# Two-layer graph network and expert layer: the path for unsorted edges left out, and the last group of nodes cut to its own rows

## The reference, cut to what matters

```python
# x (6250, 512) float32; src, dst (100000,), sorted by dst
def sage(h, W_self, W_neigh, b):
    agg = segment_sum(h[src], dst, 6250)             # 100000 rows of 512 floats are gathered
    deg = segment_sum(ones, dst, 6250)
    return relu(h @ W_self + agg / max(deg, 1) @ W_neigh + b)
x = x + sage(sage(layernorm(x), ...1), ...2)         # two layers
xf = layernorm(x)
topv, topi = top_k(xf @ Wg, 2)                       # 8 experts, 2 for each node
y_e = layernorm(relu(xf @ W1[e] + b1[e]) @ W2[e] + b2[e]) * gamma[e] + beta[e]
x = x + sum over the 2 experts of softmax(topv) * y_e
```

## Time and profile before

| | us |
|---|---|
| median of three runs | 3189.15 |
| the profiled execution | 3192.86 |
| its span | 3191.1 |
| first stage, up to the first gather | 108.9 |
| first layer, first gather to the second layer's first | 1151.6 (108.9 to 1260.5) |
| second layer, first to last gather | 1110.1 (1260.5 to 2370.6) |
| first row of the experts' stage asked for | 2417.4 |

### The profile page before, as it was taken

How to read it: one execution, slowest core, us unless ns; L and a number is a source line. 1 busy time by engine, 2 the same in 40 slices (tenths; PEclk the granted TensorE clock), 3 DMA queues, 4 the chain that set the end, 5 groups by cost and what they waited for, 6 DMA issues and landing times.

```text
span 3191.1 us, 66577 instructions
## 1 busy us (share of the span) xinstructions
PE 2713.7 (85%) x12191; PEld 2108.6 (66%) x12192; DVE 2280.9 (71%) x5226; ACT 1727.3 (54%) x3193; POOL 2189.5 (69%) x2216
## 2 busy tenths in 40 slices
PE   1488878887889987899999999999996999899997
PEld 0366666666667765677777677777774777777775
DVE  7567666766667775888888888888875666666665
ACT  3455545545556654655656566555553555555554
POOL 0577777777777776777777777777753556555665
PEclk9988888888889998989899899888887999999998
DMA  7788888778877776777777777777765554555443
GB/s 276 230 256 267 270 273 268 254 254 267 257 247 227 213 215 222 231 231 231 235 236 234 234 230 234 227 233 224 235 196 157 136 135 75 132 133 135 73 80 63
DMA packets 234835, 664.22 MB, mean 208 GB/s; under 512 B 46602, under 2 KB 48196, under 8 KB 227612
## 3 DMA queue, kind: packets, MB, share of 16 engines
q0 software_dynamic: 151712, 465.58, 52.3%
q10 hardware_dynamic: 60768, 127.43, 11.2%
q1 hardware_dynamic: 22300, 70.69, 6.1%
HBM read 551.72 MB, written 111.83 MB: 208 GB/s over the span
## 4 chain that ended last, share of the span: by engine, by line
PE 36%; POOL 28%; issue 12%; DMA 11%; ACTq 5%; DVE 4%; ACT 2%; SPq 2%; DVEq 1%; POOLq 0%
POOL store_all L685 27%; PE ps L1619 22%; PE ps L1646 6%; DMA store_all<-h_scratch,srcT 5%; PE ps L1647 4%; ACTq L375 2%; DMA out<-store_all,idx_s 2%; DMA store_all<-xn_scratch,srcT 2%; DVE r_lo L1240 1%; PE ps L1747 1%; PE ps L1759 1%; DMA m_g<-gate_scratch,idx_g 1%; ACT r_hi L834 1%; ACTq L874 1%; ACTq L868 1%
## 5 line engine op out<-in xcount | busy, mean ns | idle before, releaser
L834 ACT ACTIVATE r_hi<-store_all 128x512 fp32r x1680 | 1008.0, 626 | 747.0 <-SPq L571 406.0
L1240 DVE TENSOR_TENSOR r_lo<-store_all,r_hi 128x512 fp32r<-128x512 f32 x1680 | 1130.2, 687 | 344.7 <-ACT r_hi L834 339.7
L685 POOL DMA_INDIRECT store_all<-xn_scratch,srcT x784 | 863.2, 1101 | 274.1 <-issue 227.4
L685 POOL DMA_INDIRECT store_all<-h_scratch,srcT x784 | 872.8, 1113 | 254.2 <-issue 239.3
L1646 PE MATMUL ps<-r_hi,sel 128*128 128x512 f32 x1680 | 831.0, 495 | 94.9 <-DVE r_lo L1240 94.0
L1647 PE MATMUL ps<-r_lo,sel 128*128 128x512 f32 x1680 | 711.2, 423 | 0.0
L1646 PEld LDWEIGHTS ps<-r_hi,sel 128*128 128x128 f32 x1680 | 348.4, 207 | 229.7 <-DVE r_lo L1240 162.1
L1232 DVE TENSOR_TENSOR sel<-iota_g,dstT 128x384 fp32r (+4 forms) x602 | 317.9, 528 | 137.3 <-PE ps L1647 93.8
L1619 PE MATMUL ps<-wts,sT 128*128 128x512 f32 x1176 | 415.7, 469 | 0.0
L1647 PEld LDWEIGHTS ps<-r_lo,sel 128*128 128x128 f32 x1680 | 352.5, 210 | 21.7
L1645 PEld LDWEIGHTS ps<-ones_col,sel 128*128 128x128 f32 x840 | 173.5, 206 | 286.7 <-issue 155.1
(11 more groups left out here) (283 smaller groups left out, 3120.3 us busy)
## 6 DMA issues: line engine op xcount, KB each, us to landing
expert_weights_scratch<-w_both ACTq DMA_DIRECT2D x64, 512.0 KB, 5.2
wts<-expert_weights_scratch SPq DMA_DIRECT2D x32, 1024.0 KB, 10.3
store_all<-in_L_ffn_W ACTq DMA_DIRECT2D x64, 256.0 KB, 5.4
self_t<-xn_scratch ACTq DMA_DIRECT2D x49, 256.0 KB
store_all<-xn_scratch,srcT POOLq DMA_INDIRECT x784, 3.9
h_scratch<-x_t ACTq DMA_DIRECT2D x49, 256.0 KB
self_t<-h_scratch ACTq DMA_DIRECT2D x49, 256.0 KB
store_all<-h_scratch,srcT POOLq DMA_INDIRECT x784, 4.0
```

The source lines that it names most:

```text
L685: pool.indirect_dma_start(rows[:, t % SLOTS, :], None, rows_d, bass.IndirectOffsetOnAxis(ap=srcT[:, t:t + 1], axis=0)).then_inc(s_rows[t % ...
L834: act.activation(r_hi[:, ring(k), :], slot_of(t), ACT.Copy) \
L1240: dve.tensor_tensor(r_lo[:, ring(k), :], slot_of(t), r_hi[:, ring(k), :].bitcast(F32), ALU.subtract).then_inc(S["lo"] if k < ST else S["lo ...
```

## The change

The lap path is taken out: `in_order` and its tables, the loop over laps on GpSimd, the registers for laps on SyncE, the load of `tab_pos` on ScalarE. `tables2` runs after chunk 4 instead of chunk 5 and `tables3` after chunk 7 instead of chunk 8. GpSimd gathers 782 tiles instead of 784 in each layer, and SyncE passes on as many. The ranges of the last group are made with 6144 as its first node (`thr_lo`) instead of 6122; worked out from the seeded inputs, its first tile becomes 768 instead of 765 (it then has edges in 14 tiles), and its 17 steps run over tiles 768 to 784. Rows 6122 to 6143 are complete in group 47 alone then, so that the last group stores only the other 106 of its rows.

```diff
-BLOCKS = ET // SLOTS
-PER_LAP = ET // BATCH
-SHARED = 12
@@ layer
-                if places:
-                    t0 = value(eng, cell(places, g), NT * ET)
@@ SyncE
-            def arrived(l, before, b, j):
+            def arrived(l, b, j):
-                sp.wait_ge(s_rows[j % FLY], before + b * (16 * SLOTS // FLY) + 16 * (j // FLY + 1))
+                sp.wait_ge(s_rows[j % FLY], (b * (SLOTS // FLY) + j // FLY + 1) * 16 + l * 16 * len(range(j % FLY, TT, FLY)))
@@ freed
-                at, lap = (m, 0) if isinstance(m, int) else (within(m % PER_LAP, PER_LAP - 1), within(m // PER_LAP, NT - 1))
-                sp.wait_ge(S["lo"], packed // PACK + lap * ST)
-                sp.wait_ge(S["lox"], packed % PACK + lap * (ET - ST) + 1)
+                sp.wait_ge(S["lo"], packed // PACK)
+                sp.wait_ge(S["lox"], packed % PACK + 1)
@@ GpSimd
-                laps = pool.value_load(tab_laps[0:1, 0:1], min_val=1, max_val=NT)
-                for t in range(ET):
+                for t in range(TT):
...
-                with pool.If_lt(pool.to_reg(1), pool.to_reg(laps)):
-                    with pool.Fori(1, laps) as lap:
...
@@ ScalarE
+        def own_rows(n):
+            return slice(DUP, P) if isinstance(n, int) and n == NT - 1 else slice(0, P)
-                    act.dma_start(rows_at(res_d, n), res).then_inc(S["store"], 16)
+                    act.dma_start(rows_at(res_d, n)[own_rows(n)], res[own_rows(n)]).then_inc(S["store"], 16)
-                    act.dma_start(rows_at(xn2_d, n), xn2_t).then_inc(S["xst"], 16)
+                    act.dma_start(rows_at(xn2_d, n)[own_rows(n)], xn2_t[own_rows(n)]).then_inc(S["xst"], 16)
-                layer(act, half, hooks, tab_tile, places=tab_pos, loop_end=loop_end,
+                layer(act, half, hooks, tab_tile, loop_end=loop_end,
@@ VectorE
+            didv(dve.tensor_copy(thr_lo[:], thr_i[:]))
-            didv(dve.tensor_scalar(thr_hi[:], thr[:], float(P), None, ALU.add))
+            didv(dve.tensor_scalar(thr_hi[:], thr_lo[:], float(P), None, ALU.add))
-                t(dve.tensor_tensor(cmp_m[:], over_g(t_max[:]), over_b(thr[:]), ALU.is_lt))
+                t(dve.tensor_tensor(cmp_m[:], over_g(t_max[:]), over_b(thr_lo[:]), ALU.is_lt))
-            def in_order():
...
-                t(dve.tensor_scalar(loose[:], ps[:, 4, 3 * P:3 * P + 1], 1.0, None, ALU.min))
...
-                t(dve.tensor_tensor(in_win[:], in_win[:], over_b(in_lap[:]), ALU.mult))
@@ first stage, after chunk c
-                if c == 3:
-                    in_order()
-                if c == 5:
+                if c == 4:
                     tables2()
-                if c == 8:
+                if c == 7:
                     tables3()
```

More of the change, by code:

```diff
@@ L54 @@
 BATCH = 4
-BLOCKS = ET // SLOTS
-PER_LAP = ET // BATCH
-SHARED = 12
-assert ET % SLOTS == 0 and SLOTS % FLY == 0 and SLOTS % BATCH == 0
+assert SLOTS % FLY == 0 and SLOTS % BATCH == 0
 LAG = ST + BATCH - 1
@@ L174, in build @@
             thr = sbc(c1, "thr", [P, NT])
+            thr_lo = sbc(c1, "thr_lo", [P, NT])
             thr_hi = sbc(c1, "thr_hi", [P, NT])
@@ L182, in build @@
             end_g = sbc(c1, "end_g", [NT, 1])
[L183 to L188, removed]
             span_g = sbc(c1, "span_g", [NT, 1])
@@ L430, in within, with layer @@
             return v if isinstance(v, int) else v.with_bounds(min_val=0, max_val=top)
-        def layer(eng, step, hooks, table, places=None, opening=None, tail=None, loop_end=None, early=None, lead=0, last=0):
+        def layer(eng, step, hooks, table, opening=None, tail=None, loop_end=None, early=None, lead=0, last=0):
             back = max([d for fs in hooks.values() for _, d in fs] + [2 if early else 0])
@@ L460, in tile @@
                     with eng.Fori(0, n) as j:
-                        step(ST, g, x0 + j, within(t0 + ST + j, (NT if places else 1) * ETP - 1))
+                        step(ST, g, x0 + j, within(t0 + ST + j, ETP - 1))
                     if loop_end:
@@ L590, in _ @@
                     sp.wait_ge(s_tab, TAB_DONE)
-                blocks = sp.value_load(tab_laps[0:1, 1:2], min_val=BLOCKS, max_val=NT * BLOCKS)
-                before = blocks * (16 * SLOTS // FLY) if l else 0
                 for j in range(SLOTS):
[L594 to L597, removed]
+                    forward(l, 0, j)
+                with sp.Fori(1, TT // SLOTS) as b:
                     for j in range(SLOTS):
[L599 to L602, removed]
+                        forward(l, b, j)
+                for j in range(TT % SLOTS):
+                    forward(l, TT // SLOTS, j)
+                sp.sem_inc(L[l]["arr"], ETP - TT)
             sp.wait_ge(L[1]["dense"], NT)
@@ L695, in _ @@
                         pool.wait_ge(S["arr"], t - FLY + BATCH)
-                    gather(t)
-                with pool.If_lt(pool.to_reg(1), pool.to_reg(laps)):
-                    with pool.Fori(1, laps) as lap:
[L700 to L703, removed]
+                    pool.indirect_dma_start(
+                        rows[:, t % SLOTS, :], None, rows_d,
+                        bass.IndirectOffsetOnAxis(ap=srcT[:, t:t + 1], axis=0)).then_inc(s_rows[t % FLY], 16)
             def column(q):
@@ L1133, in tables2 @@
                                            op0=ALU.mult, op1=ALU.add), wait=False)
-                t(dve.tensor_scalar(lap_row[:], iota[0:1, 0:NT], loose[0:1, 0:1], float(ET), ALU.mult, ALU.mult))
-                t(dve.tensor_tensor(tab_pos[:], f_row[:], lap_row[:], ALU.add), wait=False)
-                t(dve.tensor_scalar(tab_laps[:, 0:1], loose[0:1, :], float(NT - 1), 1.0, ALU.mult, ALU.add), wait=False)
-                t(dve.tensor_scalar(tab_laps[:, 1:2], loose[0:1, :], float((NT - 1) * BLOCKS), float(BLOCKS),
-                                    ALU.mult, ALU.add), wait=False)
-                t(dve.tensor_scalar(in_lap[:], iota[0:EP, 0:NT], 1.0, loose[0:EP, 0:1], ALU.min, ALU.mult))
-                t(dve.tensor_scalar(in_lap[:], in_lap[:], -1.0, 1.0, ALU.mult, ALU.add))
                 over_b = lambda a: a.unsqueeze(2).to_broadcast([EP, NT, EB])
```

56 lines of the change are left out of this document (20 added, 36 removed).

## The result

The kernel after takes 3180.83 us (median of 20 runs, 3169.87 to 3191.81) beside 3189.28 for the kernel before in the same job: ratio 0.9974, 95% interval 0.9963 to 0.9985. That is 8.4 us faster where 29 were forecast, at the very upper edge of the range (3181), and no rival of mine describes it as a whole. The profiled executions lie 12.3 us apart (spans 3191.1 and 3178.8). The tile view gives the stages: first and last start of each kind of gather.

What follows compares the result with a forecast made beforehand. Layer 1's middle was taken as bound by the tiles' consumers, the rest by GpSimd's gathers; -29.8 - 4.4 - 1.2 + 0.6 + 3.0 + 2.5 = -29.3 us gave a 3160 us median, range 3147 to 3181.

Steps and rivals of the forecast that it cites:

- No `tab_pos` load, layer 1, -29.8: Layer 1, ScalarE between groups: dropping the load saves 0.96 us in each of 31 groups, 29.8 us, all on the path.
- Nothing is late in its place: Layer 1, between groups: no other wait replaces the load; rounding's buffers are free, VectorE and TensorE have their entries already.
- So it stays the slower one, but barely: Layer 1: the consumer, 23.5 us a group after the change, stays slower than GpSimd's gathers at 22.6 us.
- The cap of 34.1 us: Layer 1: GpSimd is truly held up for 34.1 us, so a faster ScalarE wins at most that.
- Rival 1, the delay moves on: Between groups: weight loads' issues wait instead of the removed load, only 17.4 us won, 3172 us; chance 0.17.
- Rival 2, the clock stays up: Layer 1: shorter pauses keep TensorE's clock at its upper level, -34.1 for -29.8, 3156 us; chance 0.10.
- Rival 3: Layer 1: denser traffic lengthens gathers by 0.08 us, deciding from 0.065; GpSimd becomes the bound, 3197 us; chance 0.05.
- Rival 4: Layer 1: the 34.1 us stay as another wait takes the place, 3190 us; chance 0.10.
- First stage, -4.4 and half of -1.2: Before layer 1: removed operations and earlier tables save 4.4 us; GpSimd's lap register load, before each layer, saves 1.2 altogether.
- Two gathers fewer, shorter arithmetic in SyncE, layer 2's loads: 0: Both layers' last gathers, SyncE's lap arithmetic, and layer 2's removed `tab_pos` loads: each worth 0 us.
- The store of 106 rows, +3.0: End of layer 1: the last store runs on two DMA engines, 3.7 us at 59 GB/s against 0.7, +3.0 us.
- The last group's window, +0.6 and +2.5: Last group: steps wait for later tiles, +0.6 us in layer 1 (bounds 0, +2), +2.5 in layer 2 (0, +4).

Runs made afterwards that it cites:

- busy_store_96_10: Kernel after plus 14 unneeded matmuls in each TensorE pause of layer 1's groups 3 to 34, last group's stores cut into 96 and 10 rows: ratio 0.9907.
- moved_store_96_10: Kernel after with ScalarE's expert-weight work moved from the group boundary into the group, last group's stores cut into 96 and 10 rows: ratio 0.9886.

## Why the prediction was wrong, step by step

- *No `tab_pos` load, layer 1, -29.8: this term failed*, with 15.6 measured (16.5 and 15.1 in the kernels that differ by the load alone). "For each group one load of 0.67 goes ... all on the path" held: 29.2 us of pauses went. The step that failed is "Nothing is late in its place": it put at nothing what TensorE does behind the pause. Its clock stayed low for longer behind the shorter pause, and that took 14.1 us of the 28.0 that TensorE stood still less. "So it stays the slower one, but barely" failed too: from 200 to 600 us GpSimd's gathers became the largest part of the chain (45.5% for 6.0%).
- *The cap of 34.1 us* took GpSimd's gathers as fixed. Without the waits for buffers (less 0.30 each) a gather cost (1132.1 - 34.1) / 781 = 1.406 us before, with 13.0 us of waits left 1.413 after, and 1.400 and 1.391 in the runs with one and three loads more, where 40 and 86 us were waited. GpSimd that waits less meets more of VectorE's subtractions: 5.5 us from before to after. That the two facts hang together so is argued from these four numbers, not isolated, and two other runs speak against a fixed rule: with no wait left a gather cost 1.406 us in busy_store_96_10 and 1.397 in moved_store_96_10. From 200 to 600 us the idle time of ScalarE that a tile's arrival ended was 40 us after and 17 before, which again shows GpSimd as the bound there.
- *Rival 1, the delay moves on*: seen (0.30 us more in the second issue), but worth little, since the load of `tab_tile` shortened by as much. That its 17.4 us for the layer lies near the measured 15.6 is luck: the pauses did lose 29.2. *Rival 2, the clock stays up*, looked at the right thing with the wrong sign: it let the clock only help. *Rival 3* was right that gathers lengthen (by 0.013 us), far under its 0.065. *Rival 4* is out.
- *First stage, -4.4 and half of -1.2*: -3.0 in all, so the size of -4.4 failed. The removed operations and the lap register are all of it; the tables' move gave nothing, which was my lower bound. The chain after runs there through a load issued at 40.18 that lands 14.15 us later.
- *Two gathers fewer, shorter arithmetic in SyncE, layer 2's loads: 0*, right (1107.1 and 1107.3).
- *The store of 106 rows, +3.0*: the mechanism was right, the size off. It took 6.62 us for 2.04, +4.6. The rate was wrong: 59 GB/s came from one microsecond of a load's tail, and while the store ran, the DMA engines moved 41 GB/s at a share of 0.13, about two of 16 engines. The 217 KB take 5.3 us at that rate, not 3.7. Why the two engines are slower here, the runs don't show. The whole boundary gave +4.8 for +3.0: the store is issued 1.35 us later behind tile 781 (17.44 for 16.09, and 18.75 in the second execution of the kernel after), it takes 4.6 longer, and layer 2's first gather follows its landing 1.1 sooner (0.26 for 1.37), where the lap register's half of -1.2 had 0.6.
- *The last group's window, +0.6 and +2.5*: 0.8 in layer 1 with the cut store's second issue of 0.36 in it, and +4.3 in layer 2, where four kernels with the window at 6122 need 47.5 to 49.9 us and six with the cut 51.7 to 54.1. A size, above my value, and 0.3 over my bound in this pair; the means of the four and of the six lie 3.9 apart, within it.

## What to carry to other kernels

A pause of TensorE has two prices, its length and the work at half clock behind it, and shortening a pause of 4.5 us to 3.5 gave back only half of the microsecond. Filling it with idle products took away most of the second price, moving the work away took away the pause, and either left GpSimd as the bound. When an engine waits for issues, look at what was issued just ahead: moving two weight stores made the loads behind them three times shorter. And before an edge case is cut to its exact rows, count what the rows do to the DMA: 106 rows cost 4.4 us more than 128, or than 96 and 10.

## What the runs showed of the hardware

- The low stretch behind a pause came in lengths of about 2.5, 4.7 and 6.5 us, to the end of whole steps of this kernel: 4.7 in 29 of 30 groups in the kernel before, mixed in the kernel after. Pauses of 2.3 us in the kernel after were followed by each of the three. The Trainium skill (TensorE: Matmul & The Clock Gate, "Part 1: The HAM clock gate") calls the window that the clock's monitor looks at free-running, and says that it isn't reset when a kernel starts. The mixed lengths agree with that; no run here shows the monitor itself.
- A gather takes 0.95 us alone and mostly up to 1.45 beside VectorE's subtraction of two tiles in SBUF (a few take up to 2.43); without it 0.981 in the mean for 1.114. The Trainium skill (GPSIMD Engine Reference, "Specifications") says that GpSimd's SBUF interfaces are shared with VectorE, with contention where its instruction has two inputs from SBUF. The run agrees.
- An SBUF word is loaded into a register in 0.27 us, and in up to 1.58 right behind two DMA issues of the same engine that move 512 KB each.
